# Where an attention stage splits a side tile: DVE and a PSUM bank, or POOL at the end of its iteration

## The reference

```python
x = x + cross_attention(norm(x), ctx, Wq, Wk, Wv, Wo, gq, gk)     # 16 heads of 128, RMS norm on q and k
x = x + gated_ffn(norm(x), W_gate, W_up, W_down, signs, scales)   # with Walsh-Hadamard transforms
x = x + state_space_scan(ctx, norm(x), ...)
x = x + top2_of_16_experts(norm(x), ...) + shared_expert(norm(x))
```

```python
q, k, v = norm(x) @ Wq, ctx @ Wk, ctx @ Wv     # 2048 columns: 16 heads of 128
q, k = rmsnorm(q, gq), rmsnorm(k, gk)
out = softmax(q @ k.T / sqrt(128)) @ v
x = x + out @ Wo
```

## Time and profile before

| | |
|---|---|
| time, median of 3 runs | 2810.0 us (2807.88 to 2812.79) |
| the profiled execution | 2818.8 us |
| its span | 2817.0 us |
| PE busy | 2322.5 us, 82% of the span |
| DVE busy | 1925.7 us, 68% |
| POOL busy | 1350.6 us, 48% |
| ACT busy | 1235.8 us, 44% |
| mean granted clock of PE | 0.904 |

### The profile page before, as it was taken

One profiled execution on the slowest core, in us unless ns is written; L12 is line 12 of the kernel. 1 busy time (PEld: TensorE's weight loads), 2 busy tenths in 40 slices (PEclk: granted clock), 3 DMA queues, 4 the chain that ended last, 5 costly groups with the idle time before them and its releaser, 6 DMA issues. The chain is left out here.

```text
span 2817.0 us, 37908 instructions
## 1 busy us (share of the span) xinstructions
PE 2322.5 (82%) x10784; PEld 1780.8 (63%) x10785; DVE 1925.7 (68%) x3625; ACT 1235.8 (44%) x2129; POOL 1350.6 (48%) x1722
## 2 busy tenths in 40 slices
PE   3799999999999999997373899898998848559981
PEld 2687878878787878885231566565665525447770
DVE  6576777777676767775952999989999974412323
ACT  2344444444444444443244665564655512024430
POOL 0233333333332333331900788888978913378424
PEclk7799999999999999998685999999999979679995
DMA  6512232321223222123136565555665311465416
GB/s 269 202 65 92 83 106 83 105 83 66 83 83 106 83 100 68 71 79 105 46 146 187 182 209 173 172 179 172 202 178 170 115 68 41 165 206 179 141 52 250
DMA packets 136940, 363.84 MB, mean 129 GB/s; under 512 B 21280, under 2 KB 58912, under 8 KB 118560
## 3 DMA queue, kind: packets, MB, share of 16 engines
q1 hardware_dynamic: 123648, 328.36, 34.7%
q0 software_dynamic: 6320, 20.71, 2.4%
q10 hardware_dynamic: 6768, 12.32, 1.1%
HBM read 290.06 MB, written 71.30 MB: 128 GB/s over the span
## 5 line engine op out<-in xcount | busy, mean ns | idle before, releaser
L1803 POOL TENSOR_TENSOR mix_drive<-mix_du,mix_rows 128x512 f32<-128x512 f32 x256 | 326.5, 1282 | 155.5 <-DMA mix_rows<-bc_d 121.0
L662 POOL TENSOR_SCALAR att_probs<-att_probs,att_recip 128x512 f32<-128x512 f32 x256 | 184.0, 723 | 402.5 <-DVE att_recip L743 397.2
L585 ACT ACTIVATE att_probs<-att_s,att_bias,att_rq 128x512 f32<-128x512 f32 x256 | 200.0, 781 | 301.2 <-DVE att_bias L739 299.0
L1856 DVE TENSOR_TENSOR_SCAN mix_state<-mix_state,mix_drive 128x512 f32<-128x512 f32 x256 | 312.6, 1221 | 15.6 <-POOL mix_drive L1803 9.7
L1687 ACT ACTIVATE mix_state<-mix_delta,mix_a 128x512 f32<-128x512 f32 x256 | 176.7, 691 | 278.2 <-DVE mix_drive L1867 237.8
L1788 POOL TENSOR_TENSOR mix_y<-mix_y,mix_drive 128x512 f32<-128x512 f32 x180 | 230.5, 1280 | 78.7 <-DVE mix_drive L1867 78.7
L1596 PE MATMUL mix_down<-mix_wd,mix_hT 128*128 128x512 f32 x512 | 232.6, 597 | 8.6 <-DVE residual_x L1887 8.6
L738 DVE TENSOR_REDUCE att_nmax<-att_s 128x1 f32<-128x512 f32 x256 | 175.0, 683 | 64.6 <-PE att_s L101 64.5
L591 ACT CAST att_pT<-att_pt 128x512 fp32r<-128x512 f32 x256 | 143.4, 588 | 142.6 <-PE att_pt L442 138.4
L789 DVE TENSOR_TENSOR att_pT<-att_pt,att_pT 128x512 fp32r<-128x512 f32 x256 | 169.5, 682 | 45.4 <-ACT att_pT L591 45.0
L99 PE MATMUL att_w<-att_w_qkv,att_cx 128*128 128x256 f32 x512 | 162.7, 318 | 35.7 <-DVE att_w_qkv L725 27.3
(11 more groups left out here) (363 smaller groups left out, 6824.4 us busy)
## 6 DMA issues: line engine op xcount, KB each, us to landing
att_xn<-normT SPq DMA_DIRECT2D x32, 2048.0 KB, 9.5
mix_gu<-guT SPq DMA_DIRECT2D x64, 1024.0 KB, 8.3
mix_rows<-bc_d SPq DMA_DIRECT2D x128, 256.0 KB, 5.2
guT<-att_ffnT SPq DMA_DIRECT2D x32, 512.0 KB, 3.4
mix_wd<-wdT SPq DMA_DIRECT2D x16, 1024.0 KB, 7.8
slots<-exp_y ACTq DMA_DIRECT2D x47, 256.0 KB, 2.0
normT<-nrm_outT SPq DMA_DIRECT2D x4, 2048.0 KB, 9.1
exp_raw<-in_L_ffn_Wg SPq DMA_DIRECT2D x16, 512.0 KB, 5.9
```

Of the source, the lines that this page charges most:

```text
L585: act.activation(probs[:, n, :], ps_s[n % 2][:, :], ACT.Exp, bias=bias[:, n:n + 1], scale=rq[:, n:n + 1], accum_out=sums[:, n:n + 1]).then ...
L662: pool.tensor_scalar(probs[:, n, :], probs[:, n, :], recip[:, n:n + 1], 1.0, ALU.mult, ALU.mult).then_inc(s_pn, 1)
L1803: pool.tensor_tensor(drive[q % RING][:, :], du[i % DUS][:, :], rows[g % ROWS][:, 0, :], ALU.mult).then_inc(s_drive, 1)
L1856: dve.tensor_tensor_scan(h[:, :], h[:, :], drive[q % RING][:, :], 0.0, ALU.mult, ALU.add).then_inc(s_scan, 1)
```

## The change

The tile of the feed-forward weights leaves the sequence of the two PSUM banks' splits. ACT copies the transposed tile back unrounded, into `fraw`, from which it was transposed (`ffn_out`), and the bank is free then. POOL makes both parts from `fraw`, in two instructions at the end of its iteration (`split_ffn`, which also has the wait for the last store of `fT`). `ffn_hi` and `ffn_lo` go. SP's load of the next `fraw` and its store of `fT` both wait for POOL's second instruction (`s_flo`). The counts of `s_pt` and `s_ptlo` go from 9 to 8 an iteration.

```diff
@@ sync
                     if not last:
-                        sp.wait_ge(s_pt, TURNS * i + TB + 1)
+                        sp.wait_ge(s_flo, i + 1)
                         load_ffn(hp + (b + 1) // B, (b + 1) % B)
-                    sp.wait_ge(s_ptlo, TURNS * i + TB + 1 + 2)
+                    else:
+                        sp.wait_ge(s_flo, i + 1)
                     store_ffn(hp, b)
@@ tensor
-                    pe.wait_ge(s_ptlo, TURNS * i + n + 1)
+                    if h and k == 1:
+                        pe.wait_ge(s_fout, i + 1)
+                    elif h and k == 0:
+                        pe.wait_ge(s_ptlo, 8 * i + TB + 2)
+                    else:
+                        pe.wait_ge(s_ptlo, 8 * i + TB * h + k + 1)
...
                 def turn_ffn(hp, i, b):
                     pe.wait_ge(s_fraw, 16 * (i + 1))
-                    pe.wait_ge(s_ptlo, TURNS * i + TB + 1)
+                    pe.wait_ge(s_ptlo, 8 * i + TB + 1)
                     for k in range(KD):
                         tr = pe.transpose(ps_pt[(b + TB) % 2][:, k, :], fraw[:, k * P:(k + 1) * P], ident_sb[:, :])
-                    tr.then_inc(s_pt, 1)
+                    tr.then_inc(s_ft, 1)
@@ scalar
-                def ffn_hi(hp, i, b):
-                    act.wait_ge(s_pt, TURNS * i + TB + 1)
-                    act.wait_ge(s_fst, 16 * (i + 1))
-                    act.copy(fT[:, 0, :, :], ps_pt[(b + TB) % 2][:, :, :]).then_inc(s_fhi, 1)
+                def ffn_out(i, b):
+                    act.wait_ge(s_ft, i + 1)
+                    act.copy(fraw[:, :], ps_pt[(b + TB) % 2][:, :, :].rearrange("p k n -> p (k n)")).then_inc(s_fout, 1)
@@ gpsimd
+                def split_ffn(i):
+                    parts = [fT[:, n, :, :].rearrange("p k n -> p (k n)") for n in range(2)]
+                    wait_apart(pool, s_fout, i + 1, s_pace)
+                    wait_apart(pool, s_fst, 16 * (i + 1), s_pace)
+                    pool.tensor_scalar(parts[0], fraw[:, :], 1.0, 1.0, ALU.mult, ALU.mult).then_inc(s_fhi, 1)
+                    wait_apart(pool, s_fhi, i + 1, s_pace)
+                    pool.tensor_tensor(parts[1], fraw[:, :], parts[0].bitcast(F32), ALU.subtract).then_inc(s_flo, 1)
+
...
                     if not last:
                         norm_q(own, j)
+                    split_ffn(i)
@@ vector
-                def ffn_lo(i, b):
-                    dve.wait_ge(s_fhi, i + 1)
-                    dve.tensor_tensor(fT[:, 1, :, :], ps_pt[(b + TB) % 2][:, :, :], fT[:, 0, :, :].bitcast(F32),
-                                      ALU.subtract).then_inc(s_ptlo, 1)
```

More of the change, by code:

```diff
@@ L267, in stage_attention @@
     ffn_d = [W.rearrange("(n p) d -> p n d", p=P) for W in (W_gate, W_up)]
-    TURNS = HP * TB + 1
     NQ, NKV = KD * W2, KC * W2
@@ L331, in stage_attention @@
         s_pace = m.sem("pace")
-        s_fraw, s_fhi, s_fst = m.sem("ffn_raw_in"), m.sem("ffn_hi"), m.sem("ffn_stored")
+        s_fraw, s_ft, s_fout = m.sem("ffn_raw_in"), m.sem("ffn_turned"), m.sem("ffn_turned_out")
+        s_fhi, s_flo, s_fst = m.sem("ffn_hi"), m.sem("ffn_lo"), m.sem("ffn_stored")
         def pairs(eng, iteration):
@@ L446, in turn_ffn @@
                     pe.wait_ge(s_fraw, 16 * (i + 1))
-                    pe.wait_ge(s_ptlo, TURNS * i + TB + 1)
+                    pe.wait_ge(s_ptlo, 8 * i + TB + 1)
                     for k in range(KD):
                         tr = pe.transpose(ps_pt[(b + TB) % 2][:, k, :], fraw[:, k * P:(k + 1) * P], ident_sb[:, :])
-                    tr.then_inc(s_pt, 1)
+                    tr.then_inc(s_ft, 1)
                 def pv(i, h):
-                    pe.wait_ge(s_ptlo, TURNS * i + (TB + 1) * h + TB + 2)
+                    pe.wait_ge(s_ptlo, 8 * i + TB * h + TB + 2)
                     d = slice(h * D, (h + 1) * D)
@@ L589, in pt_hi @@
                     n = (TB + 1) * h + k
-                    act.wait_ge(s_pt, TURNS * i + n + 1)
+                    act.wait_ge(s_pt, 8 * i + TB * h + k + 1)
                     act.copy(pT[:, 0, k, :], ps_pt[(b + n) % 2][:, :, :]).then_inc(s_pthi, 1)
-                def ffn_hi(hp, i, b):
-                    act.wait_ge(s_pt, TURNS * i + TB + 1)
-                    act.wait_ge(s_fst, 16 * (i + 1))
-                    act.copy(fT[:, 0, :, :], ps_pt[(b + TB) % 2][:, :, :]).then_inc(s_fhi, 1)
+                def ffn_out(i, b):
+                    act.wait_ge(s_ft, i + 1)
+                    act.copy(fraw[:, :], ps_pt[(b + TB) % 2][:, :, :].rearrange("p k n -> p (k n)")).then_inc(s_fout, 1)
                 def o_hi(i, h):
@@ L636, in iteration @@
                         q_parts(j, 1)
-                    ffn_hi(hp, i, b)
+                    ffn_out(i, b)
                     o_hi(i, 0)
@@ L864, in iteration @@
                         q_lo(j, 1)
-                    ffn_lo(i, b)
                     o_lo(i, 0)
```

## The result

The changed kernel takes 2909.1 us (median of 4 runs, 2906.4 to 2911.7) against 2808.9 (4 runs, 2805.6 to 2812.8): a ratio of 1.036, 95% interval 1.034 to 1.038. It is 100 us slower, where 27 were forecast and the range ended 66 above before. The profiled execution took 2906.7 us (span 2904.9), 88 more than the one of before, whose 2818.8 lay 10 above its median.

A forecast was written before the change was run, and what follows sets the result against it. The prediction took TensorE (PE), 96% busy in the attention stage, as the bound. It summed -9.7 (wait removed) + 34 (stalls) + 3 (clock) = +27 us onto 2810, giving 2837 us, range 2810 to 2876.

The forecast's parts named there:

- Moved on SP: SP's in-order queue: the xn load behind the store now waits for POOL's split, so PE stalls; 34 us.
- 30 pairs: Iterations whose xn reload waits for POOL; 20 were to stall, six over a loop end had 17.0 to 18.4 us.
- R: End of POOL's last norm_q instruction, before which the xn load could no longer be issued.
- The stalls: PE's waits for the late xn load at the query projection: 20 of them, 34 us in sum.
- X: Time from R to the xn load's arrival and PE's release: 13.8 us, of which landing 9.8.
- Q - R: Time from R to PE's first matmul of the next query projection, read from the old trace: 10.8 to 18.4 us.
- Removed from DVE: ffn_lo leaves DVE in mid-iteration, ending PE's 0.3 us wait at L442 each iteration: -9.7 us.
- The clock: PE's clock falling after its idle stretches in the attention stage: +3 us.
- Two of the three longest: Of PE's stalls on xn, those assumed to lose 1.7 us each to the lower clock: +3 us.
- each stall brings the clock down: Rival: PE's clock falls after every xn stall, 34 to 41 us more, 2868 to 2875; chance 0.12.
- A slower hand-over: Rival: DVE holds up POOL's pair, or landing is slow; X = 15, stalls 62 us, 2862; chance 0.08.
- Lands in time: Rival: the xn load still arrives before PE needs it, X below 12.5; 2800 to 2807; chance 0.07.

The follow-up runs named there:

- e4: Kernel before the change, with SP's xn load and the weights behind it made to wait for ACT's third exponential only at b = 0, the loop end: 2849.3 us.
- e2: Changed kernel with SP's xn load issued ahead of the wait for POOL's split, the weights behind it in mid-iteration: 2788.6 us, ratio 0.994.
- e3: Kernel before the change, with SP's xn load (and the weights behind it) made to wait for ACT's third exponential in every iteration: 2848.8 us.
- e6: Changed kernel with only the weight loads moved behind the next projection, out of the loop end: 2888.5 us, ratio 1.027.
- e7: e2 with the weight loads left in the hand-over at the loop end: 2814.7 us, ratio 1.000.
- e5: Kernel before the change, with DVE's ffn_lo cut to one column of each of its four blocks: 2787.4 us, ratio 0.990.
- e1: Changed kernel with POOL's split moved in front of norm_q: 2799.1 us, ratio 0.996.

## Why the prediction was wrong

The direction was right, and the mechanism that the prediction named is there: the load behind POOL's last act, 24 stalls, L442's wait gone, the pair in its hole without delay for `norm_p`. A second one, as large, was missing from it. The size was off by 73 us, in four of its steps.

**A step that was missing: the loop end.** In "Moved on SP" I followed the late load only to its reader, PE at `queries`. Six of its 30 pairs span a loop end and had 17 us and more of room, so they were counted as free. They cost 41 us, 25.6 by waits and the rest mostly at the lower clock behind them. The transfers issued at R now run while the engines go round the loop, and there PE's and DVE's "issue" waits grow (ACT and POOL have none). In the stage, in us, with what e4 has from late transfers alone:

| waits put down to issue | before | after | e4 | e2 |
|---|---|---|---|---|
| PE `att_s` and `att_w` L99 (12) | 17.5 | 41.9 | 45.8 | 21.2 |
| DVE `att_recip` (12) | 27.2 | 65.2 | 59.9 | 27.3 |

That late transfers slow the loop end is shown, by e3 and e4 one way and by e2, e6 and e7 the other. How they do it is argued only. In every kernel a loop end has nine packets of the trace's instruction queues, where the other iterations of the loop have two to five. One packet took no longer after (0.71 us on average, 0.72 before), but the packets came later: the eighth starts 16.8 us behind R before and 22.7 after. Engines that wait for fetches held up behind data would look like this, but a loop end slowed by something else would spread its packets too, and no run separates the two. The weights, which the prediction didn't price at all since they are wanted much later, are 20 us of it (e6).

**The stalls: 34 forecast, 55.7 measured.** X was right within its range: 14.2 us on average over the 24 (13.1 to 15.1), against 13.8. Its terms came out at 0.54, 0.62, 0.18, 1.29, 0.11, 1.09 and 10.35 for landing and release, so the landing carries the difference. With before's gaps this X gives 42 us of stalls, 8 of the 22 missing. POOL's pair, priced from other shapes, came to 1.91 against 1.96 us:

```profile
L698 POOL TENSOR_SCALAR att_ffnT<-att_ffn_raw x32: 617/618/622, 143.3 to 1387.8; 128x512 fp32r<-128x512 f32 x32
L700 POOL TENSOR_TENSOR att_ffnT<-att_ffn_raw,att_ffnT x32: 1280/1290/1298, 144.1 to 1388.6; 128x512 fp32r<-128x512 f32 x32
```

What failed is the other side, Q - R. I took the 24 gaps from the trace of before as they stood, 12.4 us on average. PE's own work between R and Q takes less: 11.7 in e2, and 11.85 in the changed kernel when the stall is taken off. Before's gaps were long because of the clock, though PE is at full speed from R to Q in all of them. The stretches at the lower clock lie ahead of R but behind `sums_q`, from which R follows: they make PE late at Q and leave R where it is. Behind such a stretch the gap was 13.9, 12.4 and 12.0 us on average at b = 0, 1 and 2, and without one 12.7, 11.1 and 10.8. The change takes most of these stretches away, and the gaps with them. So 24 x (14.17 - 11.85) = 55.7 us, and the other 13 of the missing 22 are this 0.55 us each.

**Removed from DVE: -9.7 forecast.** The wait went whole, as worked out. But DVE's step was worth 24 us (e5), since the stretches at the lower clock go with it. The prediction looked at the clock for what stalls would cost and took 0.98 as given, without asking what made it less than 1.00. This gain is in the changed kernel too, and hides how large its losses are: against e2, which has it, they are 120 us.

**The clock: +3 forecast, about +17 measured**, from 60 to 95 us of work at the lower level. "Two of the three longest" stalls was too few: the stalls were 2.3 us on average and not 1.7, and up to 4.4; the loop ends, which held 1.00 in the earlier trace rows, idle for longer too, and come back at 0.50. By position all of it is at the loop ends, where PE worked 7 us at the lower clock before and 47 after. Between them it is 51 and 48: behind 11 of the 24 stalls, all eight of 3.3 us or more among them, the clock fell, for 41 us of PE's work in all, and nearly all of before's own stretches are gone. That the two cancel is luck.

Of the rivals, "each stall brings the clock down" was true of 11 stalls of 24. It doesn't explain the loop ends, which have 68 of the changed kernel's 119 us at the lower clock. "A slower hand-over" is out, X = 14.2 and POOL's steps at their price; only in e1 did the split slow another engine. "Lands in time" would have needed X under 12.5, and the least of the 24 was 13.1.

On the rule of the Trainium skill for one DMA ("DMA: Bandwidth & Descriptors", "Anatomy of one DMA"), whose estimate was 6.8 us: with nothing ahead of it the same load took 7.7 (e3), with 0.75 MB about 10. Most of the difference was the queue, and what is issued ahead has to be added to the rule. That section gives its rule for DMAs on GpSimd's path, and these loads are SP's.

The version that beats both kernels is e2: the change as it is, and the `xn` load issued when its buffer comes free. At 2788.6 us it is 0.7% under before.

## What to carry to other kernels

When a change makes a wait on an in-order DMA queue later, follow every transfer behind it to its reader, and then look at what the engines do while it is in flight: at the end of this kernel's hardware loop bulk traffic cost PE and DVE idle time, so issue loads as early as their buffer allows and not in the hand-over. A gap read from a trace can be as long as it is because of the clock, also of the clock before the gap; where the granted clock is under 1.00 in a stretch, find what brings it down before reading slack from it. A short wait that repeats can be worth more than its sum.

## What the runs showed of the hardware

- A loop end took 41.2 us with no bulk load issued right ahead of it and 48.1 with 4.25 MB, and DVE's longest wait without a releaser went from 2.7 to 7.4 us (before and after). One wait more on SP, with nothing else changed, made it 47.4 and 47.3 us (e3, e4).
- PE's clock fell while PE was busy without a gap, within 0.7 us of the end of 16 matmuls of one column and 2.1 to 3.1 us behind a wait of 0.3 us: 17 times in the 30 iterations of before, and not once with DVE's step cut and the wait gone (e5).
- DVE's tensor_scalar on 128x128 went from 2.37 to 2.75 us for eight when POOL's split ran beside it on SBUF, and PE's wait for it from 2.1 to 17.7 us in the stage (e1).
